# Moving the first-half products of the last three tiles of an adapted layer behind the routing of the last tile

## What is computed

```python
x = x + ffn0(cond0(x, itok_B_1_198, ...), spline weights)          # first layer
z = x @ W.T + ((x @ A[adapter].T) @ Bm[adapter].T) * s[adapter]    # adapted layer
logits = z @ gate_w.T ; top_w, sel = top_k(logits, 2)              # routing, 8 experts
top_w = softmax(top_w)
h = silu(z @ gate_proj[e].T) * (z @ up_proj[e].T)                  # each chosen expert e
x = x + sum_e top_w[e] * (h @ down_proj[e].T)
```

## Time and profile before

| | us |
|---|---|
| runs of the kernel | 1235.79, 1236.15 (median), 1238.35 |
| the profiled execution, its own time | 1224.29 |
| its span in the trace | 1222.6 |
| first layer and weights of the second, to | 512.4 |
| adapted layer on TensorE | 512.4 to 679.5 |
| TensorE without work | 679.5 to 702.8 |
| experts | 699.9 to 1222.6 |

### The profile page before, as it was taken

How to read it: one execution, slowest core, us unless ns; L and a number is a source line. 1 busy time by engine, 2 the same in 40 slices (tenths; PEclk the granted TensorE clock), 3 DMA queues, 4 the chain that set the end, 5 groups by cost and what they waited for, 6 DMA issues and landing times. The chain is left out here.

```text
span 1222.6 us, 34935 instructions
## 1 busy us (share of the span) xinstructions
PE 1100.6 (90%) x12488; PEld 1023.2 (84%) x12489; DVE 609.3 (50%) x1163; ACT 504.3 (41%) x994; POOL 737.5 (60%) x1081
## 2 busy tenths in 40 slices
PE   2579999999999999789999279999999999999995
PEld 1579998999998998779999269989889989899994
DVE  7856777766677764335454413333333333333332
ACT  3346777766777675335444012222222222222221
POOL 4678898898998896014435225555555545555553
PEclk9879999999999999789999679999999999999998
DMA  6044455554455543644554514666565655644443
GB/s 260 30 127 156 156 206 180 180 178 170 163 202 178 177 163 118 267 160 138 174 164 116 186 36 85 144 145 174 124 164 132 153 140 145 152 80 77 78 81 56
DMA packets 65921, 177.70 MB, mean 145 GB/s; under 512 B 12656, under 2 KB 21752, under 8 KB 62304
## 3 DMA queue, kind: packets, MB, share of 16 engines
q1 hardware_dynamic: 40736, 127.65, 30.3%
q0 software_dynamic: 19200, 38.94, 17.7%
q10 hardware_dynamic: 5952, 10.65, 2.4%
HBM read 105.84 MB, written 71.38 MB: 145 GB/s over the span
## 5 line engine op out<-in xcount | busy, mean ns | idle before, releaser
L1642 POOL TENSOR_TENSOR idle<-small 128x1 f32<-128x1 f32 x284 | 93.7, 330 | 208.7 <-DMA out<-result,scatter_at 107.6
L900 POOL TENSOR_TENSOR in_lo<-inner,in_hi 128x512 fp32r<-128x512 f32 x128 | 176.5, 1379 | 40.8 <-ACT in_hi L1052 40.5
L1720 PE MATMUL banks<-slots,zt_hi 128*128 x568 | 191.2, 337 | 4.8 <-DVE zt_lo L1809 3.0
L1722 PE MATMUL banks<-slots,zt_lo 128*128 x568 | 184.2, 324 | 0.0
L1721 PE MATMUL banks<-slots,zt_hi 128*128 x568 | 183.6, 323 | 0.0
L1145 DVE TENSOR_TENSOR inner<-silu,banks 128x512 f32<-128x512 f32 x128 | 87.6, 684 | 121.3 <-ACT silu L1047 121.2
L1821 DVE TENSOR_TENSOR hid<-silu_g,banks 128x352 f32<-128x352 f32 x71 | 37.0, 521 | 209.5 <-PE banks L1722 209.5
L1665 POOL DMA_INDIRECT out<-result,scatter_at x71 | 113.7, 1602 | 23.9 <-issue 18.9
L1787 ACT ACTIVATE zt_hi<-banks 128x512 fp32r<-128x512 f32 x72 | 43.0, 598 | 171.7 <-PE banks L1709 171.7
L1720 PEld LDWEIGHTS banks<-slots,zt_hi 128*128 128x128 f32 x568 | 107.7, 190 | 7.1 <-issue 6.7
L1721 PEld LDWEIGHTS banks<-slots,zt_hi 128*128 128x128 f32 x568 | 108.3, 191 | 0.0
(11 more groups left out here) (228 smaller groups left out, 3346.6 us busy)
## 6 DMA issues: line engine op xcount, KB each, us to landing
late_dram<-split_part SPq DMA_DIRECT2D x32, 816.0 KB, 4.3
slots<-late_dram SPq DMA_DIRECT2D x24, 1088.0 KB, 6.3
raw_part<-in_late_w SPq DMA_DIRECT2D x16, 816.0 KB
x_t<-in_x_t SPq DMA_DIRECT2D x16, 512.0 KB, 3.4
x_both<-in_x_tok SPq DMA_DIRECT2D x16, 512.0 KB, 5.8
x_both<-in_x_res SPq DMA_DIRECT2D x16, 512.0 KB, 3.3
x1t_dram<-x_both SPq DMA_DIRECT2D x16, 512.0 KB, 6.0
x<-x1t_dram SPq DMA_DIRECT2D x16, 512.0 KB, 6.8
```

The costliest lines, as they stand in the source:

```text
L900: nc.gpsimd.tensor_tensor(in_lo[:, cs, :], inner[u % 2][:, :, :], in_hi[:, cs, :].bitcast(F32), ALU.subtract).then_inc(in_done, 1)
L1642: nc.gpsimd.tensor_tensor(idle[:, at:at + 1], small[:, 0:1], small[:, 0:1], ALU.add)
L1720: nc.tensor.matmul(psum[bank][:, 0:FD], zt_hi[:, k, :], w_high, start=(k == 0), stop=False)
L1722: ins = nc.tensor.matmul(psum[bank][:, 0:FD], zt_lo[:, k, :], w_high, start=False, stop=(k == DK - 1))
```

## The change

1. In tiles 5, 6 and 7 half 0 is left out of the tile's own turn. When half 1 of tile 7 is done, TensorE computes half 0 of tiles 5, 6 and 7 one after the other. `ranks(7)` and the count of tokens for each expert stand after the third of these twelve products.
2. `ranks(5)` and `ranks(6)` come in the following tile, after the part of half 1 of its subtiles 0 and 1 that needs `xa`; `enter(5)` and `enter(6)` come on VectorE in the following tile, in front of its last `low` (line 1452; there is none in tile 7).
3. Tile 7's split input and the split `xa` of tiles 6 and 7 lie in the place of the third expert's weights. Its load is therefore taken out of the adapted layer and put into the experts' block, after the first and third gathers have landed.
4. `z` of tiles 5 to 7 is stored in two DMAs each: columns 260 to 511 (1008 bytes a row) after half 1, columns 0 to 259 (1040 bytes a row) after half 0.
5. `enter` computes the shares before it waits for the ranks, and has 5 dependent steps in place of 7; `row_i`, `entry` and their semaphore are double.
6. In the experts the table's rows and its shares are sorted into two banks with a signal each; VectorE copies the rows, which let GpSimd begin, after 6 of the 12 matmuls.
7. The loops over tiles are written out. Two operands of the block computation lie in `x1` in place of `staging`, and its wait for the stores of `z` is gone.

```diff
+LATE = 2
+OWN = LNT - 1 - LATE
...
+        def split_x1(t):
+            return (x1t_hi[t % 2], x1t_lo[t % 2]) if t < LNT - 1 else lent_x1
+        def split_xa(t):
+            return (xa_hi[:, :], xa_lo[:, :]) if t <= OWN else [lent_xa[t - OWN - 1][:, l, :] for l in range(2)]
+        def halves_late(t):
+            return t >= OWN
...
-                steps(sp, body)
-                sp.wait_ge(weights_loaded, LOADS * EARLY)
-                load_expert(sp, EARLY, False)
+                for t in range(1, LNT):
+                    store_out(t)
+                    if t < LNT - 1:
+                        next_x1(t + 1)
...
+                for s in range(LSUB):
+                    transpose(0, s)
+                for t in range(LNT):
+                    adapters(t)
                     for s in range(2):
-                        if has_next:
+                        if t < LNT - 1:
                             transpose(t + 1, s)
-                        product(s, 1, range(DK))
+                        product(t, s, 1, range(DK))
                     pe.wait_ge(xa_done, t + 1)
                     for s in range(2):
-                        product(s, 1, [DK])
+                        product(t, s, 1, [DK])
+                    if t and halves_late(t - 1):
+                        ranks(t - 1)
                     for s in range(2, LSUB):
...
+                    if not halves_late(t):
+                        for s in range(LSUB):
+                            product(t, s, 0, range(DK + 1))
+                            if s == LSUB - 2:
+                                ranks(t)
+                for t in range(OWN, LNT):
                     for s in range(LSUB):
-                        product(s, 0, range(DK + 1))
-                        if s == LSUB - 2:
-                            ranks(t)
+                        product(t, s, 0, range(DK + 1))
+                        if t == OWN and s == LSUB - 2:
+                            ranks(LNT - 1)
+                            nc.tensor.matmul(psum[XA][:, 0:NE], ones[:, :], chosen[:, LSUB, :], start=True, stop=True).then_inc(counted, 1)
...
+                        if s == 2 and t and halves_late(t - 1):
+                            enter(t - 1)
+                    choose(t)
+                    if not halves_late(t):
+                        enter(t)
+                enter(LNT - 1)
...
+                sp.wait_ge(z_loaded[0], 32)
+                load_expert(sp, EARLY, False)
                 sp.wait_ge(weights_loaded, LOADS * SLOTS)
...
-                        ins = nc.tensor.matmul(psum[SORTED][:, w * COLS:(w + 1) * COLS], columns[0:rows, c, :, w], chosen_at[0:rows, c, :],
+                        ins = nc.tensor.matmul(psum[SORTED[w]][:, 0:COLS], columns[0:rows, c, :, w], chosen_at[0:rows, c, :],
                                                start=(c == 0), stop=(c == CHUNKS - 1))
-                ins.then_inc(sorted_filled, 1)
+                    ins.then_inc(sorted_filled, 1)
...
                 dve.wait_ge(sorted_filled, 1)
-                nc.vector.tensor_copy(share_of[:, :], psum[SORTED][:, COLS:2 * COLS])
-                nc.vector.tensor_copy(row_of[:, :], psum[SORTED][:, 0:COLS]).then_inc(table_ready, 1)
-                dve.wait_ge(table_ready, 1)
+                nc.vector.tensor_copy(row_of[:, :], psum[SORTED[0]][:, 0:COLS]).then_inc(table_ready, 1)
+                dve.wait_ge(sorted_filled, 2)
+                nc.vector.tensor_copy(share_of[:, :], psum[SORTED[1]][:, 0:COLS]).then_inc(shares_ready, 1)
+                dve.wait_ge(shares_ready, 1)
```

More of the change, by code:

```diff
@@ L1257, in use, with stores_of @@
             return LSUB // 2 * t + s // 2
[L1259 to L1267, removed]
+        def split_x1(t):
[4 more added lines that the diff above has]
+            return t >= OWN
+        def stores_of(b):
+            return sum(2 if halves_late(t) else 1 for t in range(b, LNT, 2))
         with nc.Block() as block:
@@ L1339, in body, with product @@
                     ins.then_inc(filled[XA], 1)
[L1341 to L1353, removed]
+                def product(t, s, half, chunks):
+                    hi, lo = split_x1(t)
+                    own_hi, own_lo = split_xa(t)
+                    bank, rows = Z[s % 2][half], slice(s * P, (s + 1) * P)
+                    if 0 in chunks:
+                        pe.wait_ge(drained[bank], use(t, s) + 1)
+                    for k in chunks:
+                        x_high, x_low = (hi[:, k, rows], lo[:, k, rows]) if k < DK else (own_hi[:, rows], own_lo[:, rows])
+                        for i, (x, w) in enumerate(((x_high, w_hi), (x_high, w_lo), (x_low, w_hi))):
+                            last = k == DK and i == 2
+                            ins = nc.tensor.matmul(psum[bank][:, 0:HALFW], x, w[:, k, half * HALFW:(half + 1) * HALFW],
+                                                   start=(k == 0 and i == 0), stop=last)
+                    if DK in chunks:
+                        ins.then_inc(filled[bank], 1)
@@ L1389, in token_rows @@
                     act.wait_ge(filled[bank], use(t, s) + 1)
-                    if s == 0 and not (isinstance(t, int) and t == 0):
+                    if s == 0 and t:
                         act.wait_ge(out_stored, 16 * t)
@@ new lines, in store @@
+                def store(t, halves, cols):
+                    for half in halves:
+                        for pair in range(2):
+                            act.wait_ge(drained[Z[pair][half]], use(t, LSUB - 1) + 2)
+                    act.dma_start(z_tiles[t][:, :, cols], z_out[t % 2][:, :, cols]).then_inc(z_stored[t % 2], 16)
+                for s in range(LSUB):
+                    high(0, s)
+                for s in range(LSUB):
+                    token_rows(0, s)
+                for t in range(LNT):
+                    if t > OWN:
+                        act.wait_ge(early_low, EARLY * (LNT - 2))
+                    act.wait_ge(drained[XA], t + 2)
+                    nc.scalar.activation(split_xa(t)[0], xa[:, :], ACT.Copy).then_inc(xa_high, 1)
+                    if t and halves_late(t - 1):
+                        shares(t - 1)
+                    if t < LNT - 1:
@@ L1529, in body @@
                                 ins = nc.vector.tensor_tensor(lo, raw, hi.bitcast(F32), ALU.subtract)
-                                if not has_next:
+                                if t < LNT - 1:
+                                    ins.then_inc(early_low, 1)
+                                else:
                                     ins.then_inc(weights_loaded, LOADS)
-                    choose(t, b)
-                    enter(t, first and b == 0)
-                for s in range(LSUB):
-                    low(0, 0, s)
-                steps(dve, body)
+                        if s == 2 and t and halves_late(t - 1):
[4 more added lines that the diff above has]
+                enter(LNT - 1)
                 places = [0]
```

162 lines of the change are left out of this document (87 added, 75 removed).

## The result

The changed kernel takes **1245.22 us** (median of 5 runs, 1241.12 to 1248.76) against 1236.15 for the kernel before in the same session: ratio **1.0087**, 95% interval 1.0068 to 1.0106. Forecast were 1230.85 and a gain of 5.3; measured is a loss of 9.1. Its profiled execution took 1241.12 with a span of 1239.3.

The account below looks back on a forecast made before the run. Bound: tile 7's routing, GpSimd's DMAs and DRAIN up to the first gather, with TensorE waiting 23.3 us. Block opening 3.45 earlier plus sorting 1.85 gave 5.3, so 1236.15 became 1230.85 us (50%); range 1226.3 to 1236.2.

Parts of the forecast that it names:

- TensorE 689.9 ... GpSimd's side is last, by 1.5: End of adapted layer: TensorE done at 689.9, last half store landed 694.7, GpSimd's side opening the block at 696.5.
- I take the shift over as it is.: Whole kernel: the profiled span's gain of 5.3 applied unchanged to the median 1236.15, 12 above the profiled execution.
- TensorE's stand for tile 7's `x1`, 6.7 (6.2 to 8.3): Tile 6: TensorE wants tile 7's input at 637.1, its load lands at 643.8, so it waits 6.7.
- The clock, 2.7 (0 to 3.4): Tile 6: TensorE at half clock after waiting for `x1`, adding 2.7; 0 if the clock holds.
- The routing of tile 7: Tile 7, adapters to entries: adapters start at 656.9, entries ready at about 674 instead of 680.8.
- GpSimd sets the block's opening: Tile 7's entries queue behind tile 6's to 689.35; landing 1.6, DRAIN 5.28; block opens at 696.5, 3.45 earlier.
- Sorting -1.85: Experts' block: six of twelve sorting matmuls (1.72) and one copy (0.15) leave the path to the first gather.
- The split stores: Rival, 10%: slow half stores of `z` delay tile 7's load and the block's opening; slower, 1239 to 1245 at worst.
- The clock did not hold: Rival, 15%: clock holds after tile 6's wait, or load little disturbed; gain 8.0 to 9.6, 1228.2 to 1226.5.
- no burst held up a gather: Rival, 17%: the third expert's load delays the fourth gather; gain only 1.3 to 3.3, about 1233.5.
- Not brought forward: Rival, 8%: block's opening stays put, for example by a longer DRAIN; only the sorting gains, 1234.3.
- the -5.3: Whole kernel: total forecast gain, 3.45 from the block's earlier opening plus 1.85 from the sorting.

Follow-up runs that it names:

- e10: The kernel before, unchanged, profiled again in the session where it takes 1234: ratio 0.9998.
- e17: The changed kernel with GpSimd holding the entries of tiles 0 to 4 until the next tile's adapters are done: 0.9981, 1232.02 us.
- e18: The changed kernel as it is, run again in a session where before takes 1236: 1.0064, 1244.21 us.
- e9: The changed kernel as it is, run again in the session where before takes 1234: 1.0072.
- e11: The changed kernel with no half 0 left for later (`LATE = 0`), everything else of the change kept; before at 1234: 1.0072.
- e16: The changed kernel with entries of tiles 0 to 4 held until the next tile's adapters, tile 5's until tile 7's; before at 1222: 1.0001.
- e5: The kernel before, unchanged, profiled once more in a session where it takes 1222: 0.9996.
- e7: The kernel before with only the sorting changed (two banks, rows first, first gather released by them); before at 1222: 0.9987.

## Why the prediction was wrong, point by point

- **"TensorE 689.9 ... GpSimd's side is last, by 1.5", with "Written-out loops, the double buffers, the shorter `enter` ...: nothing, they lie beside TensorE".** This is the step that failed: the forecast put TensorE's path together from tiles without stands and left it a margin of 1.5. TensorE's last product ends at 716.7 instead of 689.9. Of these 26.8, 11.8 are longer tiles 1 to 4, which before has as well where it takes 1234 (88.4 in e10, 89.0 here); behind the start of tile 5 come stands of 2.2, 3.1, 0.8, 2.3 and 2.7, and behind the 2.2, the 3.1 and the 2.7 the clock goes to its lower level. No term stood for them. They follow GpSimd's bursts of indirect DMAs: with the bursts of tiles 0 to 4 moved, e17 is at 0.9981 where e18 is at 1.0064. And as the new order has no room behind TensorE's last product, they count in full (90.1 from tile 5 to the block in e9 against 79.1 in e10).
- **"I take the shift over as it is."** I noted that the median lay 12 above the profiled execution. It was part of the price: it meant that the tiles timed were not the tiles traced. Which of the parts around the deferral brings e11's 9 us stays open.
- **TensorE's stand for tile 7's `x1`, 6.7 (6.2 to 8.3):** 6.03, 6.1 and 6.1 in three profiles of the changed kernel, 8.13 in e16, 7.6 in e17: from just below the range to its upper part. (The landing in the sum should read 643.5, not 643.3: 634.78 + 0.9 + 7.8.)
- **The clock, 2.7 (0 to 3.4):** in the first profile the granted clock was 0.50 from 660 to 662 and 0.98 from 662 to 664, after work began at 659.36, so about 2.7 us at the lower level, which cost 1.3. In e16 it was 0.50 or 0.51 from 642 to 652, with work from 646.64 on: 5.4 us, which cost 2.7. In range, and where nothing else stands the forecast's own number.
- **Adapters of tile 7 wait 1.1 (0 to 1.7):** 0.34.
- **The routing of tile 7.** Forecast, counted from tile 1's start at 545.4: adapters(7) after 111.5, entries(7) after 128.6. e16, free of stands: 658.96 - 546.62 = 112.3, and 677.53 + 0.17 - 546.62 = 131.1, of which 1.67 is `enter`'s wait for tile 5's entries, which that experiment held. The model of the stages was sound. In the first profile adapters(7) come after 670.48 - 545.71 = 124.8, and the 12 between are the stands and their clock.
- **GpSimd sets the block's opening.** Wrong by its consequence: TensorE ends at 716.7 instead of 689.9, and the last half store with it; GpSimd is through 4.8 before SyncE. Its own terms held: 698.36 to 709.05 for eight DMAs, 1.44 to the DRAIN (forecast 1.6), 5.28. But 1.1 of the 3.45 that the opening was to come earlier was the step from 2.7 to 1.6, and e5 and e7 have 1.8 and 1.7 with nothing changed there.
- **Sorting -1.85:** 6.78 to 4.97, and 5.00 in e7. **Third load 0:** all waits for gathers in the experts are 1.4, longest 0.5, against 3.4, longest 1.7, before.
- **The rivals.** The split stores were to be the slower case; the last one, issued at 717.17, is in by 720.6, so they are not slow. The clock did not hold, and no burst held up a gather. "Not brought forward" came closest, with the wrong cause. No rival had an event of all tiles: all looked at tiles 6 and 7 and behind, where the change was meant to act.
- **Is the -5.3 there without the stands?** Only partly tested. e16 is 1.0001, with tile 5's entries held about 4 longer than needed; the unheld changed kernel never met a session at 1222. In e16 the block opens 156.8 after tile 1's start, where it is 154.5 in the profile before and the forecast was 151.1. By e16's rows an opening some 3 earlier without that hold is my estimate, which would leave a gain near 3. This stays open.

## What to carry to other kernels

When a kernel's median does not match its traced execution, the trace does not yet show what is timed: get a second profile before pricing an edit by it. Work that is "beside" the bottleneck still has a place in time; ask for each engine whose bursts the edit shifts, which signals of the bottleneck fall into them. Here one wait on an idle engine was worth 10 to 12 us, twice what the whole rearrangement aimed at. And a rearrangement that takes the idle time out of the bottleneck's path takes away its room as well: stands that lay in front of a long wait anyway count in full from then on. So compare both kernels stage by stage on one occasion before a loss is put down to something that both have.

## What the runs showed of the hardware that was not expected

On the occasions where before takes 1234 to 1236, a copy that waits for TensorE's last matmul of a product starts up to 5 us late while GpSimd issues its eight indirect DMAs of 0.96 each; at 1222 it is on time with the same burst beside it. The first ones do little harm: in e17 the burst starts 3.7 to 3.8 into a tile, two of its DMAs have begun before the matmul, and the copies at 7.1 are on time. Later copies then meet the rest of the burst, but have 1.4 of room, and tiles of 20.0 to 20.8 instead of 19.3 remain. Whether TensorE's signal travels late or the matmul itself ends late cannot be told from the trace, where the ends of matmuls are modelled. What sets the two kinds of occasions apart is open too: nothing that was changed here switches between them, one chip had both, and a run of the unheld changed kernel at 1222 is missing. The traces themselves tell them apart. Those of the 1222 sessions, and the one that the prediction rests on, hold 7010 to 7062 records of DMA landings, those of the others 5733 to 5976, with no case between. Whether that has to do with the late copies no run shows.
